# Two chained attention blocks on eight images: the first two images reordered, and eight roundings moved from ScalarE to GpSimd

## What is computed

```python
# block 0
q, k = Wq @ x + bq, Wk @ x + bk            # 32 channels
v = Wv @ x + bv                            # 256 channels
x = gamma * (v @ softmax(q.T @ k).T) + x
# block 1
h = group_norm(x) * norm_w + norm_b        # 32 groups
q, k, v = q_w @ h + q_b, k_w @ h + k_b, v_w @ h + v_b
x = x + proj_w @ (v @ softmax(q.T @ k / 16).T) + proj_b
```

## Time and profile before

| | |
|---|---|
| three runs | 809.24, 810.87, 812.41 us; median 810.87 |
| the profiled execution | 809.52 us, of which its span is 807.7 |
| mean granted clock of TensorE | 0.994 of full speed |
| busy: TensorE, VectorE, ScalarE, GpSimd | 778.9, 555.6, 468.6, 160.4 us |
| TensorE idle before its first matmul | 9.1 us |

### The profile page before, as it was taken

How to read it: one execution, slowest core, us unless ns; L and a number is a source line. 1 busy time by engine, 2 the same in 40 slices (tenths; PEclk the granted TensorE clock), 3 DMA queues, 4 the chain that set the end, 5 groups by cost and what they waited for, 6 DMA issues and landing times.

```text
span 807.7 us, 9687 instructions
## 1 busy us (share of the span) xinstructions
PE 778.9 (96%) x3756; PEld 641.0 (79%) x3756; DVE 555.6 (69%) x790; ACT 468.6 (58%) x605; POOL 160.4 (20%) x144
## 2 busy tenths in 40 slices
PE   5799899999999999999999999999999999999998
PEld 4578778887788878888788877888778888887886
DVE  4855766878568785787757785577856855575564
ACT  4774764568555675557745686455855566444342
POOL 4800051023100231002310042102310024103300
PEclk9999999999999999999999999999999999999999
DMA  5100001002000030001100011000100000000101
GB/s 182 53 0 2 1 4 50 0 2 76 30 0 1 1 105 0 1 1 53 53 0 1 1 53 52 2 1 1 53 0 1 1 27 26 0 1 1 52 1 53
DMA packets 10365, 18.98 MB, mean 23 GB/s; under 512 B 2128, under 2 KB 3920, under 8 KB 10320
## 3 DMA queue, kind: packets, MB, share of 16 engines
q1 hardware_dynamic: 10320, 18.36, 6.5%
HBM read 9.97 MB, written 8.39 MB: 23 GB/s over the span
## 4 chain that ended last, share of the span: by engine, by line
PE 82%; DVE 11%; ACT 5%; issue 2%; DMA 1%; SPq 0%; ACTq 0%; DVEq 0%
PE ring L543 25%; PE ring L545 25%; PE ring L544 25%; PE ring L553 4%; PE ring L563 3%; DVE h_lo L904 2%; DVE pt_lo L1007 2%; DVE res L1043 2%; DVE q L968 1%; ACT prob L763 1%; DVE neg_raw L992 1%; ACT prob L760 1%; DVE neg_max L990 1%; ACT pt_hi L774 1%; DVE k L960 1%
## 5 line engine op out<-in xcount | busy, mean ns | idle before, releaser
L543 PE MATMUL ring<-pt_hi,v_hi 128*128 128x512 f32 x512 | 203.2, 397 | 0.6 <-DVE pt_lo L1010 0.6
L545 PE MATMUL ring<-pt_hi,v_lo 128*128 128x512 f32 x512 | 201.5, 394 | 0.0
L544 PE MATMUL ring<-pt_lo,v_hi 128*128 128x512 f32 x512 | 201.4, 393 | 0.0
L763 ACT ACTIVATE prob<-ring,neg_max 128x1024 f32<-128x1024 f32 x64 | 71.5, 1118 | 160.3 <-DVE neg_max L993 160.3
L463 POOL TENSOR_TENSOR v_lo<-v_f,v_hi 128x512 fp32r<-128x512 f32 x32 | 43.2, 1349 | 428.7 <-ACT v_hi L801 428.7
L992 DVE TENSOR_REDUCE neg_raw<-ring 128x1 f32<-128x1024 f32 x64 | 78.3, 1224 | 71.6 <-PE ring L545 71.5
L543 PEld LDWEIGHTS ring<-pt_hi,v_hi 128*128 128x128 f32 x512 | 96.9, 189 | 21.7 <-issue 1.6
L545 PEld LDWEIGHTS ring<-pt_hi,v_lo 128*128 128x128 f32 x512 | 96.8, 189 | 21.3
L544 PEld LDWEIGHTS ring<-pt_lo,v_hi 128*128 128x128 f32 x512 | 97.0, 189 | 18.8
L1007 DVE TENSOR_TENSOR pt_lo<-prob,pt_hi 128x1024 fp32r<-128x1024 f32 x64 | 83.1, 1298 | 33.1 <-ACT pt_hi L774 32.9
L990 DVE TENSOR_REDUCE neg_max<-ring 128x1 f32<-128x1024 f32 x64 | 77.8, 1222 | 37.6 <-PE ring L553 37.4
(11 more groups left out here) (133 smaller groups left out, 1218.0 us busy)
## 6 DMA issues: line engine op xcount, KB each, us to landing
out_y<-res SPq DMA_DIRECT2D x32, 256.0 KB, 2.2
x_in<-in_x SPq DMA_DIRECT2D x7, 1024.0 KB, 4.9
x_in<-in_x SPq DMA_DIRECT2D x2, 512.0 KB, 4.9
h_f<-in_wv_t SPq DMA_DIRECT2D x1, 256.0 KB, 5.2
res<-in_wq SPq DMA_DIRECT2D x1, 256.0 KB, 6.4
res<-in_wk SPq DMA_DIRECT2D x1, 256.0 KB, 6.7
res<-in_wv SPq DMA_DIRECT2D x1, 256.0 KB, 6.9
res<-in_wp_t SPq DMA_DIRECT2D x1, 256.0 KB, 7.0
```

Of the source, the lines that this page charges most:

```text
L543: mm(out, w_hi, m_hi, start=first, stop=False)
L544: mm(out, w_hi, m_lo, start=False, stop=False)
L545: return mm(out, w_lo, m_hi, start=False, stop=last)
L763: activation(prob[:, p % PROBS], ring[:, slot], ACT.Exp, bias=neg_max[:, k % 2:k % 2 + 1], accum_out=row_sum[:, k % 2:k % 2 + 1]).then_inc ...
```

## The change

It does these things:

- TensorE begins with 30 matmuls of `ones` by `ones` (fp32, 128 columns) into slot 3 (`keep_busy`), as soon as GpSimd has set `ones`.
- The loads of the two small biases move behind those of image 0, with a semaphore of their own (`bqk_loaded`).
- In `opening`, TensorE makes `shift` before the values tile (0, 2); VectorE makes `shifts(0)` before both key parts; ScalarE's key part of (1, 0) moves behind the exponent of keys tile 0.
- GpSimd waits for `shift_ready` before `bias_rows`, and `split_weights` moves to the end of its start.
- The high parts of image 0's eight keys tiles are made by GpSimd (`first_prob_hi`), the first two inside `residual0(0)`, two among the roundings of image 2. ScalarE's `prob_hi` leaves them out; VectorE waits on `p_hi0` for them.
- The bias products move from step 5 of image 0, slot 0, to s10, slot 3.
- In the second image, scores tiles (2, 0) to (2, 2) move from `early` to `late`, value tile (2, 1) from s6 to s7, and the banks before the sides change in s2, s4, s5 and s7. In s4 VectorE takes the low part of the tile first.

```diff
-PLACE = {("qk", 1, 0): 2, ("value0", 0, 2): 3, ("bias", 0, 0): 0}
+PLACE = {("qk", 1, 0): 2, ("value0", 0, 2): 3, ("bias", 0, 0): 3}
...
-    opening.sides = tiles("qk", 1, (0, 1)) + tiles("value0", 0, (2,))
-    opening.late = tiles("shift", 0, (0,))
+    opening.sides = tiles("qk", 1, (0, 1))
+    opening.late = tiles("shift", 0, (0,)) + tiles("value0", 0, (2,))
...
-    steps[5].sides = tiles("bias", 0, (0,))
...
     s9.late = tiles("keys", 1, (0,))
+    s10.sides = tiles("bias", 0, (0,))
...
     s2, s3, s4, s5, s6, s7, e8, e9, e10 = steps
-    s2.banks_first = 0
+    s2.banks_first = 2
     s2.sides = tiles("value0", 1, (3,))
     s2.statistics = (0, 0), (0, 1)
     s3.sides = tiles("qk", 2, (0,))
+    s4.banks_first = 3
     s4.sides = tiles("qk", 2, (1,)) + tiles("norm", 0, (0,))
-    s5.early = tiles("scores", 2, (0,))
+    s4.low_first = True
+    s5.banks_first = 2
     s5.sides = tiles("value0", 2, (0,)) + tiles("norm", 0, (1,))
-    s6.early = tiles("scores", 2, (1,))
-    s6.sides = tiles("value0", 2, (1,))
+    s5.late = tiles("scores", 2, (0,))
+    s6.late = tiles("scores", 2, (1,))
     s6.hidden = s7.hidden_lo = 0
-    s7.early = tiles("scores", 2, (2,))
+    s7.banks_first = 4
+    s7.sides = tiles("value0", 2, (1,))
+    s7.late = tiles("scores", 2, (2,))
     e8.banks_first = 4
     e8.sides = tiles("query", 0, (0,))
...
-                    ("wqk_loaded", ((wqk_f, by_tile(wqk_t)), (bqk_s[:], bqk), (bk0_s[:], bk0))),
+                    ("wqk_loaded", ((wqk_f, by_tile(wqk_t)),)),
                     ("x0_loaded", ((x_in[0][:, :, half_cols[0]], x_v[0][:, :, half_cols[0]]),)),
                     ("x_loaded0", ((x_in[0][:, :, half_cols[1]], x_v[0][:, :, half_cols[1]]),)),
+                    ("bqk_loaded", ((bqk_s[:], bqk), (bk0_s[:], bk0))),
                     ("wv0_loaded", ((wv0_f, by_tile(wv0_t)), (bv0_s[:], bv0), (gamma_s[:], gamma),
                                     (ident_s[:], ident))),
...
+            def first_prob_hi(k):
+
+                p = TILE_NO["keys", 0, k]
+                if p >= PT:
+                    name, n = values_done(TILE_OF[p - PT])
+                    pool.wait_ge(S[name], n)
+                pool.wait_ge(S["keys_exp"], k + 1)
+                G.tensor_copy(pt_hi[p % PT][:], prob[:, p % PROBS]).then_inc(S["p_hi0"], 1)
+
             def residual0(i):
                 if i > 0:
                     pool.wait_ge(S["res1_ready"], i)
                     pool.wait_ge(S["h_hi"], CT * i)
                 for ct in range(CT):
+                    if i == 0:
+                        first_prob_hi(ct)
                     last = G.tensor_scalar(x1[:, ct], x_in[i % 2][:, ct], unit[:], gbv[:, ct:ct + 1],
                                            ALU.mult, ALU.add)
                 last.then_inc(S["res0_ready"], 1)
...
+            pool.wait_ge(S["shift_ready"], 1)
             bias_rows()
             pool.wait_ge(S["x0_loaded"], 16)
             pool.wait_ge(x_loaded[0], x_loads(0))
             residual0(0)
-            split_weights()
+            for k in (2, 3):
+                first_prob_hi(k)
             pool.wait_ge(x_loaded[0], x_loads(2))
             pool.wait_ge(S["ring_ready"], RING_NO["value0", 0, 3] + 1)
             for half in range(HALVES):
+                first_prob_hi(4 + half)
                 G.tensor_copy(x_hi[:, :, half_cols[half]],
                               x_in[0][:, :, half_cols[half]]).then_inc(S["x_hi"], 1)
+            for k in (6, 7):
+                first_prob_hi(k)
+            split_weights()
...
+            def keep_busy(out, passes):
+
+                for _ in range(passes):
+                    mm(out[:, 0:P], ones[:], ones[:], start=True, stop=True)
...
+            wait("ones_ready", 1)
+            keep_busy(ring[:, 3], 30)
             for now in STEPS:
...
             def prob_hi(tile):
                 kind, i, k = tile
                 p = TILE_NO[tile]
+                if kind == "keys" and i == 0:
+                    return
...
             def query_part(entry):
                 _, i, m = entry
+                if i == 0 and m == 0:
+                    act.wait_ge(S["bqk_loaded"], 16 * 2)
                 act.wait_ge(S["ring_ready"], RING_NO[entry] + 1)
...
                 shift_rows(("shift", 0, 0))
-                key_part(("qk", 1, 0))
...
                 if now.rest:
-                    key_part(("qk", 1, 1))
+                    for m in range(2):
+                        key_part(("qk", 1, m))
                     project_hi(("value0", 0, 2))
                     project_hi(("value0", 0, 3))
...
-                dve.wait_ge(S["wqk_loaded"], 16 * 3)
+                dve.wait_ge(S["wqk_loaded"], 16)
...
             def key_part(entry):
                 _, i, m = entry
+                if i == 0 and m == 0:
+                    dve.wait_ge(S["bqk_loaded"], 16 * 2)
                 dve.wait_ge(S["ring_ready"], RING_NO[entry] + 1)
...
             def opening():
-                key_part(("qk", 1, 0))
                 shifts(0)
-                key_part(("qk", 1, 1))
+                for m in range(2):
+                    key_part(("qk", 1, m))
...
-                dve.wait_ge(S["p_hi"], p + 1)
+                if p < TILES:
+                    dve.wait_ge(S["p_hi0"], p + 1)
+                else:
+                    dve.wait_ge(S["p_hi"], p - TILES + 1)
...
-                first = [entry for entry in now.sides if entry[0] in ("qk", "norm")]
+                first = [entry for entry in now.sides if entry[0] in ("qk", "norm", "bias")]
+                if now.low_first:
+                    prob_lo(now.tile)
                 for entry in first:
-                    if entry[0] == "qk":
+                    if entry[0] != "norm":
                         follow(entry)
...
-                elif now.tile:
+                elif now.tile and not now.low_first:
```

More of the change, by code:

```diff
@@ L45, in __init__ @@
         self.statistics = self.evacuate = self.evacuate_at_once = None
-        self.take_weights = self.opening = self.rest = False
+        self.take_weights = self.opening = self.rest = self.low_first = False
     def entries(self):
         return [self.tile] * bool(self.tile) + self.early + self.sides + self.late
-PLACE = {("qk", 1, 0): 2, ("value0", 0, 2): 3, ("bias", 0, 0): 0}
+PLACE = {("qk", 1, 0): 2, ("value0", 0, 2): 3, ("bias", 0, 0): 3}
 PLACE.update({("weights", 0, m): 3 for m in range(4)})
@@ L253 @@
     "ring_ready", "scores_max", "scores_exp", "log_ready", "shift_ready", "shift_read",
-    "keys_exp", "logits_max", "logits_exp", "inv_ready", "p_hi", "p_split", "tile_done",
+    "keys_exp", "logits_max", "logits_exp", "inv_ready", "p_hi0", "p_hi", "p_split", "tile_done",
     "pv_ready", "pv_read", "qk_hi", "qk_split", "value0_taken", "value0_first", "value0_hi", "value0_split", "query_hi", "query_split",
@@ L258 @@
     "layer0_split", "v0_weights", "small_ready", "ones_ready", "key_hi", "link", "pool_link",
-    "wqk_loaded", "wv0_loaded", "weights_loaded", "x_loaded0", "x_loaded1", "x0_loaded", "y_stored")
+    "wqk_loaded", "bqk_loaded", "wv0_loaded", "weights_loaded", "x_loaded0", "x_loaded1", "x0_loaded", "y_stored")
 def build(nc, x, wqk_t, bqk, bk0, wv0_t, bv0, gamma, norm_w, norm_b, wq, bq, wk, bk, wv, bv, wp_t, bp,
```

## The result

| | before | after |
|---|---|---|
| median of the runs, us | 809.24 (7 runs, 808.47 to 812.41) | 805.61 (7 runs, 802.79 to 806.73) |
| ratio of the times, 95% interval | | 0.9942 (0.9925 to 0.9959) |
| profiled execution, and its span, us | 809.52, 807.7 | 806.54, 804.7 |
| mean granted clock | 0.994 | 0.994 |

The change gains 0.6%, or 3.6 us. The seven runs after fall into two groups: three at 802.79 to 802.91 with a mean granted clock of 0.997 or 0.998, four at 805.61 to 806.73 with 0.993 to 0.995.

A forecast was written before the change was run, and what follows sets the result against it. TensorE, busy 96% of the span, was taken as the bound. Gains of 3.1 us to step 4 and 3.1 for the bias products, less 3.0 for the second image, gave 3.2 us: 806.3 like the profiled execution, median 807.0, range 801.0 to 811.5.

The forecast's parts named there:

- The start: Opening: 30 products end at 10.0 us, the query product runs at full clock, first scores come 0.9 us earlier.
- behind VectorE's three operations a half: Opening: query product ends at 12.9 instead of 14.4; after VectorE's work on each half, first scores gain 0.9 us.
- The shift: Opening of image 0: shift operations no longer held by GpSimd, key part later; 3.3 us gained, plus 0.5 for the clock.
- Low part 1 is on the path: Image 0, tile 1: VectorE's low part is held for GpSimd's residual; exponent 2 at 41.9, 3.7 us gained, 4.7 if unheld.
- idle 3.6 us: Image 0, 39.3 to 42.9 us: TensorE idles, half clock follows, and values product 1 ends 1 us later.
- Rival 3: GpSimd and VectorE hold each other on every tile of image 0; 3 us go, 809 to 811; chance 0.15.
- Bias products: Moved from step 5 to s10: 5.2 us out, 1.0 comes back, 1.1 for half clock; net gain 3.1 us.
- half clock behind them: 1.7 at two chances in three, 1.1: Behind the bias products in s10: a half-clock stretch costing 1.7 us, weighted by its chance to 1.1.
- The second image: Steps to s7: gain 1.4 to s6, then waits of 1.6 and 1.9 us; 2.0 net cost plus 1.0 for half clock.
- Rival 2: The chain in s6 and s7 is shorter than worked out and the clock holds; 801.2 to 803; chance 0.25.
- Rival 4: TensorE's savings at start and bias become waits on exponents, VectorE-ScalarE setting steps 2 to 8; 808 to 810; chance 0.11.
- Rival 5: Slower: fp32 `keep_busy` does not raise the clock, query product stays at half clock; 811.3, up to 813; chance 0.07.

The follow-up runs named there:

- experiment 1: The changed kernel with image 0's eight high parts back on ScalarE; 804.15 us, ratio 0.9920 to the kernel before.
- experiment 6: The changed kernel with 18 fp32 products at the start instead of 30; 802.94 us, ratio 0.9912 to the kernel before.
- experiment 2: The changed kernel without `keep_busy`, the 30 fp32 products at the start; 805.03 us, ratio 0.9934 to the kernel before.
- experiment 5: The changed kernel without GpSimd's wait for `shift_ready`; 804.39 us, ratio 0.9934 to the kernel before.
- experiment 11: The kernel of experiment 9 with image 0's high parts back on ScalarE; 802.60 us, ratio 0.9912 to the kernel before.
- experiment 7: The changed kernel with ScalarE's `hidden(0)` ahead of the late sum of scores (2, 1) in s6; 802.54 us, ratio 0.9915 to the kernel before.
- Experiment 4: The changed kernel with the second image's order as before (scores tiles early, value tile (2, 1) in s6); 801.48 us, ratio 0.9893 to the kernel before.
- experiment 12: The kernel of experiment 10 with bias products of 128 columns (two for the value bias); 800.83 us, ratio 0.9883 to the kernel before.
- experiment 9: The changed kernel with the second image's scores tiles early as before and 18 products at the start; 803.15 us, ratio 0.9918 to the kernel before.
- experiment 10: The kernel of experiment 9 with scores (2, 0) made inside s5 behind value tile (2, 0); 803.70 us, ratio 0.9918 to the kernel before.
- experiment 8: The changed kernel with the bias products early in step 2 of image 0 instead of s10; 809.27 us, ratio 0.9984 to the kernel before.

## Why the prediction was right, and where it was not

The predicted median of 807.0 lies 1.4 us over the measured 805.61, and the measured time in the range; the likeliest of the cases (804 to 809) came in. The sum that it was built on, 3.2 us, is what the profiled execution shows as well. But the agreement is luck: the terms were 3.1 to step 4, 3.1 for the bias products and -3.0 for the second image; measured were 4.5, 0.4 and -1.8, and the errors cancelled.

- **The start** was priced at 0.9 and gave 0.4 at the first scores. Two things were off. The products ended at 10.19 instead of 10.0, since the clock rose later than in the other six executions with 30 products; over all seven the gain is 0.4 to 1.3 us, 0.9 in the mean. And "behind VectorE's three operations a half" failed: with the query product at full clock its halves end 1.4 us apart, but VectorE needs 2.3 us for each (start 11.95 to 16.54 without a pause), so the second half waits for the first. Before, the halves came 2.6 us apart and VectorE idled 0.25 between them. It was the first half that mattered, and that one came only 0.1 us earlier. Where the image did enter at 10.0 (experiment 1), the first scores gained 0.6 us, not 0.9. "Moves up 1.0 us" failed as well: ScalarE's first rounding of image 0 came at 6.40 instead of 6.66 (in experiment 6 at 5.83). `keep_busy`, priced as the source of the gain, shows no gain in the medians at 30 products (experiment 2) and brings 1.2 us more at 18 (experiment 6). The 5.25 us to the rise of the clock was the value of one execution: with 30 products it was 3.4 to 5.2.
- **The shift.** Both tiny operations went to 0.17, the shift was ready 3.7 us earlier, 0.4 of it from the start, which leaves the 3.3 of the forecast, and exponent 0 gained 4.1 of the 4.7 predicted; the 0.6 missing are the start's 0.5 and little else. The cause given for the two long operations, GpSimd's work under them, fits all rows, though the new wait was not needed for it (experiment 5). No run put that work back under them or undid the new order of the opening, so this term, the largest, rests on the timelines alone.
- **GpSimd and VectorE.** "Low part 1 is on the path" and held for the residual: this step failed. The two operations do exclude each other, but the one held was GpSimd's (2.26 and 2.28 us), and exponent 2 came at 41.0, not 41.9; so 4.6 gained here instead of 3.7. With that, step 4 had 4.5 where 3.1 was forecast: most of the 1.4 is the 0.9 of the hold. The rest is the idle time: "idle 3.6 us", with half clock and 1 us of loss behind it, was 0.62 us, and the clock had fallen earlier, at 36.94, where TensorE had to wait in any case. The Trainium skill, SBUF — State Buffer, "Who interferes with whom", lets issue order decide who blocks. The trace agrees with the exclusion: 2.26 us is nearly 1.19 and 1.23 in a row. It cannot show the order: GpSimd's records start first each time, by 0.05 to 0.1 us, and twice GpSimd's is the long one and twice VectorE's: two later low parts, at 48.9 and 54.8, took 2.03 us beside the roundings of image 2, which TensorE's work covered, as argued. Rival 3 is refuted: it wanted this at every tile.
- **High parts.** "In itself this is even" was right, and is the answer to half of the change's name: nothing in either direction within some 2 us (experiments 1 and 11).
- **Bias products.** 5.2 out was right (4.9 at keys (0, 6)). "So 1.0 comes back" was right too, but "half clock behind them: 1.7 at two chances in three, 1.1" was mis-sized: 4.3 us came back. The stretch at half clock was 6.8 us long, of which 1.0 in the last products; the time lost in it is half its length, 3.4 us, not 1.7. In experiment 5, profiled without a stretch there, keys (1, 0) to (1, 3) take 9.31 us against 8.11 before, so 1.2 come back. What was worth 3.1 on paper was 0.4 in the profiled execution. In an execution without that stretch it is about 3.4 us more, which is the distance between the two groups of runs (802.9 and 805.6 or more); that the fast ones had none there is likely by their mean clock and not shown. Experiments 5 and 7, profiled without it, had spans of 801.2 and 799.4 us.
- **The second image.** Gain to s6 1.3 (predicted 1.4). The chain of maximum, sum, exponent, low part was worked out as 1.6 and 1.9 us of waits; they were 1.29 and 1.49. The half clock at 1.0 behind them did not come. So from keys (1, 3) to the end of s7 the loss is 1.8 us, where the forecast had 2.0 and 1.0 for the clock. Experiment 4 shows that the reordering costs 1.6 us of waits net, 1.9 by the tiles' starts, as "2.0 net" said, and experiment 7 that 1.5 of it is one entry on ScalarE.
- **Rival 2** holds the faster group of runs by its number (its 801.2 to 803 holds their 802.8 to 802.9), by half of its mechanism: the clock held, but both waits of the chain were there. Rivals 4 and 5 are refuted by keys (0, 6), 9.4 us earlier, and by the clock at 6.2 us.

Still open: what the new order of the opening is worth with all else kept; whether GpSimd's share is worth 1 us either way; why the clock falls behind the narrow products in some executions and not in others of one kernel; whether it is their width that held it in experiment 12; and whether another length of the opening, between 18 and 30 products with the weights loaded earlier, would give the gains of experiments 6 and 12 together with that of 7. That was not tried.

## What to carry to other kernels

Take the value of a moved piece from the tile that starts behind it, and price the clock with it: here a 3.5 us piece of narrow matmuls was followed, in three of ten profiled executions, by a loss as large as the piece. Where TensorE has to wait in any case, as around 37 us, half clock costs nothing. One profiled execution is one draw: before a difference of 1 or 2 us is put down to an edit, compare stretches that both kernels run alike, as the start here. A block of work put in to raise the clock should end when the data arrives, and what comes earlier for it must have its own loads in time. Where an order is written for one engine, look at which entry the next engine then puts first: one 2.4 us entry on ScalarE was most of what the reordering of the second image cost.

## What the runs showed of the hardware

- **The bias products and the clock.** Ten kernels have the one-column products in s10, run without idle time. In seven of their profiled executions the clock fell to half at 76.3 to 79.5 us, inside the products or up to 0.7 us behind them, for 3.4 us (experiments 2, 4, 9, 10) or 6.8 us (the kernel after, 6, 11); in three it stayed at full (1, 5, 7). In experiment 8 it had fallen just ahead of them and stood at half for 13.65 us, of which the last 5.8 were products of 512 columns; the kernel after, with those products in that place, was back at full after 3.4 us. With 128 columns at the same spacing of 0.44 us the one profiled execution ran on at full clock, and the mean clock of all five was 0.997 or more (experiment 12). Whether their width is the cause is not shown.
- **Idle time need not lower the clock.** It held over 1.29 us behind 18 products (experiment 6), and over 1.29 and 1.49 us in s7.
- **A stretch can be 0, 3.4 or 6.8 us** for the same instructions in the same order, as behind the bias products above.
- **Start of the clock.** fp32 products of 128 columns raised it as the three-part products do. From the first matmul to the rise it took 3.3 to 5.6 us in the fourteen profiled executions; 5.26 and 5.04 in the two without `keep_busy`.
